# Four gated attention and feed-forward layers: some norms move to ScalarE, norms move in among the residual rows, and TensorE's fillers are cut

## The reference, cut to what matters

```python
x = x + tanh(g_xattn[0]) * L0_xattn(layernorm(x), ctx)    # elu+1 features, linear attention, a second layer norm inside
x = x + tanh(g_ffn[0])   * L0_ffn(layernorm(x))           # 8 experts, top 1
x = x + tanh(g_xattn[1]) * L1_xattn(layernorm(x), ctx)    # 16 heads over 64 context rows
x = x + tanh(g_ffn[1])   * L1_ffn(layernorm(x))           # all 8 experts summed, silu gate
x = x + tanh(g_xattn[2]) * L2_xattn(layernorm(x), ctx)
x = x + tanh(g_ffn[2])   * L2_ffn(layernorm(x))           # 8 experts, top 1
x = x + tanh(g_xattn[3]) * L3_xattn(layernorm(x), ctx)    # 16 heads, as L1, with another mask
x = x + tanh(g_ffn[3])   * L3_ffn(layernorm(x))           # 8 experts, top 2

layernorm(x) = (x - mean(x)) / sqrt(var(x) + 1e-5)        # along the 256 values
```

## Time and profile before

| | us |
|---|---|
| median of 3 timed runs | 1984.73 |
| lowest, highest | 1983.77, 1984.8 |
| the profiled execution's own time | 1994.02 |
| its span (first to last instruction) | 1992.3 |

### The profile page before, as it was taken

How to read it: one execution, slowest core, us unless ns; L and a number is a source line. 1 busy time by engine, 2 the same in 40 slices (tenths; PEclk the granted TensorE clock), 3 DMA queues, 4 the chain that set the end, 5 groups by cost and what they waited for, 6 DMA issues and landing times.

```text
span 1992.3 us, 35047 instructions
## 1 busy us (share of the span) xinstructions
PE 1859.3 (93%) x11598; PEld 1565.3 (79%) x11598; DVE 1408.0 (71%) x2393; ACT 1084.1 (54%) x1979; POOL 732.1 (37%) x754
## 2 busy tenths in 40 slices
PE   7889996999999999999999999999988997897993
PEld 4679996777888888888888888888766997686993
DVE  3867776778777777777777777777766664766674
ACT  4447773665555555555555555555424774573771
POOL 6014431465354343443534435434002232352231
PEclk9999998999999999999999999999989999899997
DMA  4156662000100000000000000031104541203544
GB/s 125 35 164 193 193 187 86 2 17 17 33 31 16 32 16 32 32 16 32 26 21 32 16 32 32 16 102 59 35 35 144 149 146 47 74 2 112 172 144 140
DMA packets 113579, 138.96 MB, mean 70 GB/s; under 512 B 15332, under 2 KB 101606, under 8 KB 113504
## 3 DMA queue, kind: packets, MB, share of 16 engines
q1 hardware_dynamic: 105952, 121.70, 19.7%
q0 software_dynamic: 7552, 16.24, 2.7%
HBM read 117.22 MB, written 24.90 MB: 71 GB/s over the span
## 4 chain that ended last, share of the span: by engine, by line
PE 81%; DVE 10%; ACT 4%; issue 3%; DMA 2%; ACTq 0%; POOL 0%; SPq 0%; DVEq 0%; POOLq 0%; another core or an unknown queue 0%
PE ps L685 44%; PE ps L943 10%; PE ps L944 10%; PE ps L945 10%; PE ps L692 2%; PE ps L879 1%; ACT ps L1574 1%; DVE xs L1772 1%; DVE bn L1692 1%; ACT wsplit L1535 1%; DVE lnx L1681 1%; PE ps L1143 1%; PE ps L1102 1%; DVE wsplit L2141 1%; DVE h_lo L2122 1%
## 5 line engine op out<-in xcount | busy, mean ns | idle before, releaser
L685 PE MATMUL ps<-h_hi,wsplit 128*128 128x512 f32 (+3 forms) x2016 | 589.0, 350 | 1.8 <-DVE xT L1908 1.3
L685 PEld LDWEIGHTS ps<-h_hi,wsplit 128*128 128x128 f32 x2016 | 366.8, 188 | 48.4 <-DVE xT L1908 1.7
L685 PE MATMUL ps<-h_lo,wsplit 128*128 128x512 f32 (+3 forms) x1008 | 352.2, 349 | 0.0
L571 POOL TENSOR_TENSOR wsplit<-wraw,zero 128x256 fp32r<-128x256 f32 (+2 forms) x160 | 151.2, 962 | 498.6 <-PE ps L945 409.0
L1456 ACT ACTIVATE lnx<-ps 128x512 f32<-128x512 f32 x384 | 229.4, 598 | 107.2 <-PE ps L945 63.7
L685 PE MATMUL ps<-xTh,wsplit 128*128 128x256 f32 (+2 forms) x992 | 255.5, 311 | 15.1 <-DVE h_lo L2122 12.0
L1908 DVE TENSOR_TENSOR xT<-xT,ps 128x1024 f32<-128x1024 f32 x124 | 151.5, 1222 | 121.8 <-PE ps L685 121.8
L1465 ACT ACTIVATE h_act<-h_act 128x512 f32<-128x512 f32 x192 | 120.8, 629 | 207.6 <-DVE h_act L1886 207.5
L1469 ACT ACTIVATE h_hi<-ps 128x512 fp32r<-128x512 f32 x256 | 152.6, 596 | 146.3 <-PE ps L685 145.1
L2122 DVE TENSOR_TENSOR h_lo<-ps,h_hi 128x256 fp32r<-128x256 f32 (+2 forms) x248 | 117.7, 475 | 154.8 <-ACT h_hi L1578 143.7
L1895 DVE TENSOR_TENSOR ps<-h_act,ps 128x512 f32<-128x512 f32 x256 | 177.5, 694 | 45.1 <-PE ps L945 31.0
(11 more groups left out here) (287 smaller groups left out, 3613.6 us busy)
## 6 DMA issues: line engine op xcount, KB each, us to landing
wraw<-in_L_w SPq DMA_DIRECT2D x124, 512.0 KB, 3.6
wraw<-in_L_ffn_Wg SPq DMA_DIRECT2D x32, 256.0 KB, 2.7
wraw<-in_L_ffn_Wu SPq DMA_DIRECT2D x32, 256.0 KB, 3.0
wraw<-in_L_ffn_Wd SPq DMA_DIRECT2D x32, 256.0 KB, 3.5
x_tok<-lnx SPq DMA_DIRECT2D x12, 512.0 KB, 3.8
lnx<-y_tok SPq DMA_DIRECT2D x12, 512.0 KB, 5.9
y_tok<-lnx SPq DMA_DIRECT2D x3, 2048.0 KB, 14.0
wat<-in_attn SPq DMA_DIRECT2D x16, 256.0 KB, 4.9
```

Of the source, the lines that this page charges most:

```text
L571: return pool.tensor_tensor(out_, in_, zero[:, :].to_broadcast(shape), ALU.add)
L685: return pe.matmul(out_, lhsT, rhs, start=start, stop=stop)
```

## The change

Names new in the diff: `nmr` holds minus mean times rstd; `shift(n, g)` makes it on VectorE (one small instruction for a group); `norm_tiles(k, a, b)` on ScalarE writes `lnx` for tiles a to b-1 as rstd·x + nmr. The fourth group's norm stays on VectorE.

1. First attention: the rstd of group 3 stands ahead of `features(0)`; `query(1)` stands ahead of the products of keys and values; fillers go from 16 to 10, and from 22 each to 12, 0, 8 and 14, with 8 new ones ahead of `query(0)`; ScalarE norms groups 0 to 2 for the feed-forward block.
2. Both 16-head attentions: moments and norm of a group stand among the `add_rows` of later groups; fillers go from 30 and 32 to 14, 8, 6 and 10; TensorE runs `query(0)` and `scores(0)` ahead of turning group 1; the copies and rstds on ScalarE are interleaved.
3. End of the second attention: moments of groups 0 to 2 stand ahead of step 13, three rstds in it, `shift` behind it; ScalarE norms tiles 0 to 11 during and after steps 14 and 15; VectorE norms only tiles 12 to 15.

```diff
@@ TensorE, attn0
+                fill(7, 8)
                 pe.wait_ge(in_wat, 64)
                 query(0)
...
-                fill(7, 16)
+                fill(7, 10)
+                query(1)
                 pe.wait_ge(a0_k, 2)
...
-                query(1)
                 for s in range(NG):
                     numerator(s)
                     if s + 2 < NG:
                         query(s + 2)
-                    fill(7, 22)
+                    fill(7, A0_FILLS[s])        # (12, 0, 8, 14)
                     project(s)
@@ TensorE, mha
-                pe.wait_ge(x_done, NT * n - 4)
-                fill(0, 30)
+                pe.wait_ge(x_done, NT * (n - 1) + GROUP + 2)
+                fill(0, 14)
@@ ScalarE
+            def norm_tiles(k, a, b):
+                for i in range(a, b):
+                    act.wait_ge(nmr_done, (NG - 1) * k + i // GROUP + 1)
+                    act.activation(lnx[:, i, :], xs[:, i, :], ACT.Identity, bias=nmr[:, i:i + 1], scale=st_rstd[:, i:i + 1]).then_inc(ln_done, 1)
@@ ScalarE, attn0, in the loop over s
                     group_rstd(NG + 2 * s, s)
+                    if s > 0:
+                        norm_tiles(0, GROUP * (s - 1), GROUP * s)
@@ ScalarE, mha, step
                         exps(i + 1, 1 - j)
+                    if rstds:
+                        for g in range(NG - 1):
+                            norm_rstd(n + 1, g)
+                    if norms:
+                        norm_tiles(1, *norms)
                     inverse(i)
@@ VectorE
+            def shift(n, g):
+                four = slice(g * GROUP, (g + 1) * GROUP)
+                dve.wait_ge(std_done, norm_no(n, g) + 1)
+                dve.scalar_tensor_tensor(out=nmr[:, four], in0=mv[:, four, 0], scalar=-1.0, in1=st_rstd[:, four],
+                                         op0=ALU.mult, op1=ALU.mult).then_inc(nmr_done, 1)
@@ VectorE, attn0, in the loop over s
-                    if s > 1:
-                        norm_group(1, s - 2)
                     residual(s)
+                    if s > 0:
+                        shift(1, s - 1)
@@ VectorE, mha
                 for g in range(NG):
-                    add_rows(layer - 1, n - 1, g)
+                    add_rows(layer - 1, n - 1, g, split=True)
                     if g > 0:
-                        norm_moments(n, g - 1)
+                        norm_group(n, g - 1)
                 next_stats(n - 1, NT - 1)
                 norm_moments(n, NG - 1)
-                norm(n)
                 bounds_of_mask()
+                norm_group(n, NG - 1)
```

More of the change, by code:

```diff
@@ L63 @@
 LAG = 3
+A0_FILLS = (12, 0, 8, 14)
 MAX_TILES = 32
@@ L123, in build @@
         item_expert = sb("item_expert", [P, NT], I32)
+        nmr = sb("nmr", [P, NT])
         r_m, r_s, r_k = (sb(n, [P, NT]) for n in ("r_m", "r_s", "r_k"))
@@ L916, in mha @@
                 query(0, True)
+                scores(0, True)
+                fill(7, 8)
+                turn_group(n, 1)
+                fill(7, 6)
                 turn_group(n, 2)
-                scores(0, True)
                 turn_group(n, 3)
@@ L1404, in inverse, with step @@
                     act.activation(rden[:, :, :], rden[:, :, :], ACT.Exp, scale=-1.0).then_inc(m_rs, 1)
-                def step(i, j, queries=True, more=True):
+                def step(i, j, queries=True, more=True, rstds=False, norms=None):
                     if queries:
@@ L1423, in mha @@
                     step(i + 1, 0)
[L1424 to L1429, removed]
+                soon = layer == 1
+                step(NT - 3, 1, rstds=soon)
+                step(NT - 2, 0, queries=False, norms=(0, 2) if soon else None)
+                step(NT - 1, 1, queries=False, more=False, norms=(2, 6) if soon else None)
+                if soon:
+                    norm_tiles(1, 6, 3 * GROUP)
+                    norm_rstd(n + 1, NG - 1)
             def ffn1(n):
@@ L1780, in add_rows @@
                         next_stats(n, i - 1)
+                    if split and g > 0 and i % GROUP == 0:
+                        norm_moments(n + 1, g - 1)
             def mha(layer, m, n):
@@ L1855, in mha @@
                     step(i + 1, 0)
+                soon = layer == 1
+                if soon:
+                    for g in range(NG - 1):
+                        norm_moments(n + 1, g)
                 step(NT - 3, 1)
+                if soon:
+                    for g in range(NG - 1):
+                        shift(n + 1, g)
                 step(NT - 2, 0, ahead=False)
                 step(NT - 1, 1, ahead=False)
-                for g in range(NG - 1):
-                    norm_moments(n + 1, g)
+                if not soon:
+                    for g in range(NG - 1):
+                        norm_moments(n + 1, g)
                 residual(NT - 1)
@@ L1863, in mha @@
                 norm_moments(n + 1, NG - 1)
+                if soon:
+                    dve.wait_ge(ln_done, NT * (n + 1) + 3 * GROUP)
+                    norm_group(n + 1, NG - 1)
             def ffn1(n):
-                norm(n)
                 def x_sum(i, tp):
```

16 lines of the change are left out of this document (9 added, 7 removed).

## The result

The changed kernel takes **1973.28 us** (median of 5 runs, 1970.96 to 1976.14) against 1984.73 for the kernel before (5 runs beside it, 1983.75 to 1986.19). The ratio is 0.9942, 95% interval [0.993, 0.9953]: 11.5 us or 0.58% faster. The forecast was 1969.9, in a range of 1966 to 1978. The profiled execution took 1972.97 (span 1971.2).

What follows compares the result with a forecast made beforehand. The prediction had 81% of the span hanging on TensorE, so the change could pay only at block boundaries. Its terms, 5.7 + 3.0 + 2.1 + 4.0 = 14.8, taken from 1984.73 gave 1969.9 us, range 1966 to 1978.

Steps and rivals of the forecast that it cites:

- First attention: First attention up to the copies: copies start at 82.5 instead of 88.23, 5.7 us sooner, bounds 3.0 to 7.0.
- First half: First attention up to the first numerator: without the 6.16 wait, the numerator starts 3.5 us sooner, at 34.3.
- Fillers: First attention's projections: fewer fillers give 1.1 us ahead of the first, 2.6 less 0.5 ahead of the second.
- VectorE from there to the copies: First attention: +2.6 us for two norms off VectorE, −1.3 for waits in `shift`, −2.2 for rstd and tiles before copies.
- Start of the second attention: Second attention's head: both `bound`s about 0.9 us sooner, the fillers' 2.07 gone, so 3.0 gained, bounds 1.0 to 3.7.
- rival C: Heads and first attention: with fewer fillers TensorE's clock stays at 1.2 GHz, net +3.9 us, 1988.6; chance 0.06.
- The recorded sign of being wrong: Heads of the attentions: a granted clock of 0.5 between the head's turnings would show the forecast wrong.
- Start of the fourth: Fourth attention's head: no gain on VectorE, only the fillers' 2.07 goes, so 2.1 us, bounds 0.5 to 2.5.
- End of the second attention: From the second attention's last steps to the next block's first product: 445.0 against 449.03, 4.0 us, bounds 2.5 to 4.4.
- Everything behind follows: Behind the first attention's copies: router and first expert move sooner with the copies, giving nothing back.
- rival A: Heads: they give only what VectorE gives; the fillers' 2.07 come back in steps 0 and 1; 10.7 us, 1974.0; chance 0.15.
- Rival B: First attention and second's end: ScalarE late, tiles at 0.82, every `shift` exposed; 9.9 us gained, 1974.8; chance 0.12.

Runs made afterwards that it cites:

- e2: Kernel before with only the change's part at the starts of the second and fourth attention: 1982.66 us, ratio 0.9988.
- e3: Kernel before with only the change's part at the end of the second attention: 1978.18 us, ratio 0.9967.
- e6: Changed kernel with 22 fillers ahead of each of the first attention's four projections again: 1977.74 us, ratio 0.9959.
- e5: Changed kernel with the first attention's norms of groups 0 to 2 back on VectorE: 1971.9 us against 1985.91, ratio 0.9934.
- e7: Changed kernel with fillers behind the first attention shifted: 46 ahead of the first logits, 4 and 10 instead of 20 and 20 ahead of later turnings: 1966.75 us, ratio 0.9907.
- e11: Changed kernel with the edits of e7 and e5 together: 1983.07 us against 1999.36, ratio 0.9923.
- e9: Changed kernel with VectorE's last four norms at the second attention's end written as scalar_tensor_tensor: 1985.30 us against 1999.36, ratio 0.9939.
- e12: Changed kernel measured again without an edit: 1983.90 us against 1999.36, ratio 0.9922.
- e8: Changed kernel with shifted fillers behind the first attention, and 26 plus 13 more fillers in the heads: 1965.69 us, ratio 0.9898.

## Why the prediction was right, and where it was not

**First attention, 5.7.** Right in sum. The copies stand at a mean of 88.0 in the three traces without the part (before, e2, e3) and at 81.6 in the eight with it that keep its norms and fillers: 6.4, though the two groups range over 3.3 and 5.5 us, most of it from the time of the first numerator. *First half*, 3.5 forecast: the first numerator is at 37.6 on the mean of those three and 34.3 on that of the eleven with the new order, 3.3. *Fillers*, 3.2: 3.15 (e6). *VectorE from there to the copies*, +2.6 − 1.3 − 2.2 = −0.9: it is 0.0 (e5), since the first two terms gave 2.0 in place of 1.3, with a wait in the first `shift` alone; the last one gave −2.0. That these norms end VectorE's work 2.0 sooner behind the copies stands in no term, and neither does the cost of the 20 and 20 fillers there, which hid it (e7, e11). The step did not ask either what the new wait of 1.43 ahead of the numerator does to the clock; it costs 1.7 in 3 of 11 traces.

**Start of the second attention, 3.0.** This step failed. With the clock at 1.00 from the third turning on it gave 2.1 at best (24.52 and 24.53), with the late fall −0.2 at query 2 (26.9) and, counted to the product with 4.3 for the end, 115.0 − 111.7 − 4.3 = −1.0. The mean over the eight traces without added fillers is 25.7, a gain of 1.1. Two things were off. The first `bound` came 19.22 after the row in place of 19.34, 0.1 and not 0.9 sooner: its wait of 0.95 went, but VectorE spends 0.30 on the fourth rstd and the rest on the broken-up order. And rival C, held at 0.06 as a whole, happened in part, though neither where nor at the price it said. Its test was the clock when group 1 is turned. There it read 1.00 in the three traces that lost (after, e5, e6): the clock fell later, in the gap ahead of the fourth turning, to which the cut fillers gave no cover. And it read 0.50 there in four others (e7, e9, e11, e12), which still gained 0.7 to 2.1, where rival C had a loss of 4.5. The recorded sign of being wrong, a clock of 0.5 between the head's turnings, did show.

**Start of the fourth, 2.1.** Measured 1.5 without a late fall (25.19 against 26.67), 0.3 and −0.5 with one (e9, e2), 1.0 on the mean of the eight. The 2.07 went as forecast; the first `bound` came 0.5 later (19.89 after the row, 19.36 before).

**End of the second attention, 4.0.** Measured 4.25 (e3) and 4.33 (e2 against e12). The reasoning by GpSimd's rows held: the four tiles took 4.26.

**Everything behind follows.** Right: 27.7 to 28.8 from the copies to the first gather in all traces with the old fillers there, with and without the part, and 212.2 to 212.9 through the experts in the nine traces from the one after to e8.

The sum by the means is 6.4 + 1.1 + 1.0 + 4.3 = 12.8, inside the 11.5 ± 2.3 measured; the forecast's 14.8 lies a little outside it, and the two heads, 5.1 forecast and 2.1 measured, are why. The time of 1973.28 is near rival A's 1974.0, but not for its reason: rival A would have had the fillers' 2.07 come back in the steps, and in e2 1.95 of the 2.14 gained at query 2 still stand at the product. Rival B is out: tiles at 0.51, one `shift` with a wait.

## What to carry to other kernels

When fillers are cut, look at every idle gap that the cut leaves ahead of real work, not at the first one only: the same code here gained 2 us or lost 1 (counted to the next block's first product) depending on whether TensorE's clock fell in a gap of 1.7 us ahead of the last turning or not. When a place is made faster, look at once at the fillers behind it: those that delayed the last turning by 2.4 us before delayed it by 4.6 after, and hid what the faster place had won. When marks of two traces are compared, count both from an event that they share, not from the program's start (e11). And separate the parts of a change by marks in the traces: with a scatter of 2 us in the whole time, a mark read to 0.1 us tells apart what five rounds don't.

## What the runs showed of the hardware

The granted clock fell from 1.00 to 0.50 in the second attention's head (windows above) in a gap of 1.71 us, with one of 1.36 and a turning ahead of it. In the same code it fell at another place in e12, where it was back in time, and in e2 it did not fall again in that attention. So one profile of such a stretch is a sample and not a reading.

VectorE's norm of a tile, its operands in SBUF, ends only after GpSimd's running row does, in both forms tried: 4.26 and 4.68 for four tiles, one tile per GpSimd row. The first form takes 1.4 for four without GpSimd (1.38 at 86.46 in the trace after); the second wasn't measured alone. A row of `bn_stats` with one input (0.43, at 427.74 beside GpSimd's 1.89 from 426.34) and a residual with one operand in PSUM (0.48) were not held. The Trainium skill says this (SBUF — State Buffer, SBUF: two separate sides): the port pair that VectorE and GpSimd share is an exclusive lock for a whole instruction, which VectorE needs in a two-port mode or, against a GpSimd instruction that reads SBUF, with two SBUF inputs; whichever starts first has it and the other blocks. By that rule e9 could not gain, and the traces agree: its tiles end 0.28 after GpSimd's rows.
